# Moving the last step's burst of value products and sum products behind slot 15 of an attention kernel, with part of VectorE's end work moved forward and one key chunk's addition moved from the matrix engine to the adders

## The reference, cut to what matters

```python
Q, K, V = (split_heads(x @ W.T + b) for W, b in ((Wq, bq), (Wk, bk), (Wv, bv)))   # x: 8 x 512 x 512, 16 heads of 32
cQ = Q + split_heads(cond @ Wq.T + bq)           # cond: one row of 512 for each batch
cK = K + split_heads(cond @ Wk.T + bk)
attn = softmax(cQ @ cK.T / sqrt(32))             # 512 x 512 for each of 8 x 16 heads
out = x + attn @ V                               # float32 throughout
```

## Time and profile before

| | |
|---|---|
| median of three runs | 641.79 us |
| the profiled execution | 641.36 us |
| its span, first to last instruction | 639.5 us |
| granted TensorE clock over the span | 1.000 |
| PE busy | 633.6 us (99%) |
| DVE busy | 541.9 us (85%) |
| POOL busy | 490.6 us (77%) |
| ACT busy | 391.2 us (61%) |

### The profile page before, as it was taken

One profiled execution on the slowest core, in us unless ns is written; L12 is line 12 of the kernel. 1 busy time (PEld: TensorE's weight loads), 2 busy tenths in 40 slices (PEclk: granted clock), 3 DMA queues, 4 the chain that ended last, 5 costly groups with the idle time before them and its releaser, 6 DMA issues.

```text
span 639.5 us, 10063 instructions
## 1 busy us (share of the span) xinstructions
PE 633.6 (99%) x3528; PEld 439.5 (69%) x3528; DVE 541.9 (85%) x818; ACT 391.2 (61%) x684; POOL 490.6 (77%) x204
## 2 busy tenths in 40 slices
PE   8999999999999999999999999999999999999997
PEld 6787677666677666677666677666777666776542
DVE  7887888888888898888888888888888888998696
ACT  6466566666566666567666566565666555564773
POOL 7348877778877778877778877778877778666992
PEclk9999999999999999999999999999999999999999
DMA  8944434455434565334565334565334665424501
GB/s 262 264 101 118 116 102 114 121 151 150 108 106 106 132 151 149 103 105 102 146 151 138 105 102 108 150 152 134 101 102 117 150 166 135 117 69 120 148 17 67
DMA packets 48243, 80.83 MB, mean 126 GB/s; under 512 B 9545, under 2 KB 9801, under 8 KB 48073
## 3 DMA queue, kind: packets, MB, share of 16 engines
q1 hardware_dynamic: 47837, 80.04, 48.3%
q10 hardware_dynamic: 356, 0.16, 0.1%
HBM read 19.95 MB, written 8.39 MB: 44 GB/s over the span
## 4 chain that ended last, share of the span: by engine, by line
PE 98%; DVE 1%; DMA 0%; ACT 0%; POOLq 0%; issue 0%; DVEq 0%; ACTq 0%
PE bank L351 27%; PE bank L444 19%; PE bank L426 18%; PE bank L464 18%; PE bank L399 14%; PE bank L495 1%; DMA cond<-condT 0%; PE bank L472 0%; DVE bank L746 0%; PE bank L376 0%; POOLq L81 0%; DVE Xl L717 0%; ACT Xh L589 0%; DVE rr L784 0%; DVE rr L795 0%
## 5 line engine op out<-in xcount | busy, mean ns | idle before, releaser
L642 ACT ACTIVATE Pt<-bank 128x512 f32<-128x512 f32 x512 | 302.0, 600 | 224.0 <-PE bank L444 156.7
L746 DVE TENSOR_REDUCE mf<-bank 128x1 f32<-128x512 f32 x496 | 330.7, 684 | 59.6 <-PE bank L426 57.7
L954 POOL TENSOR_TENSOR A<-A,Pt 128x2048 f32<-128x2048 f32 x59 | 271.3, 4598 | 4.6
L444 PE MATMUL bank<-Qs,Ks 128*128 128x512 f32 x496 | 195.1, 399 | 0.1
L426 PE MATMUL bank<-Ks,Qs 128*128 128x512 f32 x496 | 194.5, 393 | 0.2
L954 POOL TENSOR_TENSOR A<-Pt 128x2048 f32<-128x2048 f32 x30 | 138.4, 4613 | 25.6 <-DVE part_sums L771 20.1
L444 PEld LDWEIGHTS bank<-Qs,Ks 128*128 128x128 f32 x496 | 92.6, 188 | 48.3 <-ACT Pt L642 26.2
L464 PE MATMUL bank<-Pt,V 128*32 128x512 f32 x1024 | 119.0, 596 | 0.0
L426 PEld LDWEIGHTS bank<-Ks,Qs 128*128 128x128 f32 x496 | 93.0, 188 | 24.0 <-DVE bank L746 3.0
L351 PE MATMUL bank<-Xh,Wh 128*128 128x512 f32 x256 | 99.8, 390 | 0.3 <-ACT Wh L581 0.3
L351 PE MATMUL bank<-Xl,Wh 128*128 128x512 f32 x256 | 100.0, 391 | 0.0
(11 more groups left out here) (74 smaller groups left out, 392.8 us busy)
## 6 DMA issues: line engine op xcount, KB each, us to landing
Qs<-hi SPq DMA_DIRECT2D x60, 256.0 KB
Ks<-hi SPq DMA_DIRECT2D x60, 256.0 KB, 3.9
Qs<-lo SPq DMA_DIRECT2D x30, 256.0 KB
Ks<-lo SPq DMA_DIRECT2D x30, 256.0 KB, 3.9
xr<-xT SPq DMA_DIRECT2D x28, 256.0 KB, 2.7
res<-xT SPq DMA_DIRECT2D x28, 256.0 KB, 2.9
outT<-ot SPq DMA_DIRECT2D x28, 256.0 KB, 3.5
Qs<-mt SPq DMA_DIRECT2D x122, 4.0 KB
```

Source lines behind the costliest of these rows:

```text
L444: e.matmul(st_bank(u)[:, :], k[:, j, kc * P:(kc + 1) * P], q[:, j, :], start=True, stop=True).then_inc(t_st, 1)
L642: e.activation(exponentials(g)[:, kc, j, :], st_bank(u)[:, :], ACT.Exp, scale=SCALE).then_inc(a_e, 1)
L746: e.reduce_max(to[:, 4 * j + qc:4 * j + qc + 1], MXB[u % 2][:, :], AXX).then_inc(v_mx, 1)
L954: e.tensor_tensor(sums, ex[:, 0, :, :] if kc == 1 else sums, ex[:, kc, :, :], ALU.add).then_inc(p_a, 1)
```

## The change

Six things are changed.

1. The burst in step 31 (values of chunks 0 and 1, sums of step 30) stands behind the scores of slot 15 in place of slot 12's.
2. `last_sums(30)` is one chunk's products in place of two: all four chunks are added up before it. To that end DVE adds chunks 0 and 1 of step 30 (`add_first(30)`, right behind the turned maxima of step 31), and POOL adds chunks 2 and 3 to it, waiting for DVE (`v_a`). POOL has two additions for step 30, as before.
3. `last_sums(31)` takes the chunks in the order 2, (0+1), 3 in place of (0+1), 2, 3.
4. PE's totals of step 27 move from slot 13 of step 30 to slot 2 of step 29, between the values of chunks 0 and 1.
5. DVE's finish of step 27 moves to step 29, slot 2, and
6. its key sums of step 28 to step 29, slot 12. Both stood behind the last reduction.

```diff
--- before.py
+++ after.py
@@ -70,11 +70,11 @@
 
 END_VALUES_AT = ((2, 12), (13,), (1, 8))
 END_TURN_AT = 2
-END_SUMS_AT = 12
-POOL_ADDS = 2
+END_SUMS_AT = 15
+END_FINISH_AT, END_KEY_SUMS_AT = 2, 12
 END_BANKS = ((1, 4, 3), (2, 12, 4))
 LAST_EARLY = (0, 1)
-LAST_ORDER = (0, 2, 3)
+LAST_ORDER = (2, 0, 3)
 
 
 def cond_attention(nc, xT, condT, wqT, wkT, wvT, biasT, outT):
@@ -481,22 +481,19 @@
 
             def last_sums(g, parts):
 
+                e.wait_ge(v_f, finished(G - 3, FIN if g == G - 1 else 1))
                 for kc in parts:
-                    if kc == 0:
-                        if g == G - 1:
-                            e.wait_ge(v_f, finished(G - 3, FIN))
-                            e.wait_ge(v_a, 1)
-                        else:
-                            e.wait_ge(v_f, finished(G - 3, 1))
-                            e.wait_ge(p_a, 3 * g + POOL_ADDS)
+                    if kc == 0 and g == G - 1:
+                        e.wait_ge(v_a, 2)
+                    elif kc == 0:
+                        e.wait_ge(p_a, 3 * g + 2)
                     else:
                         e.wait_ge(a_e, st_unit(g, kc, 3))
                     for j in range(4):
                         m = e.matmul(sums_bank(g)[32 * j:32 * j + 32, :], ones[:, :],
                                      added_up(g)[:, j, :] if kc == 0 else exponentials(g)[:, kc, j, :],
-                                     start=(kc == 0), stop=(kc == KC - 1))
-                if KC - 1 in parts:
-                    m.then_inc(t_l, 1)
+                                     start=(kc == parts[0]), stop=(kc == parts[-1]))
+                m.then_inc(t_l, 1)
 
 
             warm_up()
@@ -557,11 +554,17 @@
                     elif i < 0:
                         pass
                     elif i == 0 and n == END_VALUES_AT[i][0]:
-                        values(t - 1, (0, 1, 2, 3) if len(END_VALUES_AT[i]) == 1 else (0, 1))
+                        values(t - 1, (0,))
+                        e.wait_ge(v_mx, u - 1)
+                        totals(G - 5, MXB[u % 2])
+                        held = G - 5
+                        values(t - 1, (1,))
+                    elif i == 1 and n == END_VALUES_AT[i][0]:
+                        values(t - 1, range(KC))
                     elif n == END_VALUES_AT[i][0]:
                         values(t - 1, (0,))
                         end_totals(t - 3)
-                        values(t - 1, (1, 2, 3) if len(END_VALUES_AT[i]) == 1 else (1,))
+                        values(t - 1, (1,))
                     elif n in END_VALUES_AT[i] and t < G - 1:
                         values(t - 1, (2, 3))
                     elif n in END_VALUES_AT[i]:
@@ -570,7 +573,7 @@
                         values(t - 1, (3,))
                     if t == G - 1 and n == END_SUMS_AT:
                         values(G - 1, LAST_EARLY)
-                        last_sums(G - 2, (0,) + tuple(range(POOL_ADDS + 1, KC)))
+                        last_sums(G - 2, (0,))
             last_sums(G - 1, LAST_ORDER)
             values(G - 1, tuple(range(len(LAST_EARLY), KC)))
 
@@ -785,10 +788,12 @@
                 e.wait_ge(v_s, g + G - 1)
                 e.reciprocal(rc[:, :], rr[:, :].rearrange("p (n i) -> p n i", i=32)[:, :, 0]).then_inc(v_f, 1)
 
-            def add_first():
-                e.wait_ge(v_s, 2 * (G - 3))
-                e.wait_ge(a_e, st_unit(G - 1, 1, 3))
-                e.tensor_tensor(added_up(G - 1), Pt2[:, 0, :, :], Pt2[:, 1, :, :], ALU.add).then_inc(v_a, 1)
+            def add_first(g):
+
+                e.wait_ge(v_s, 2 * (g - 2))
+                e.wait_ge(a_e, st_unit(g, 1, 3))
+                ex = exponentials(g)
+                e.tensor_tensor(added_up(g), ex[:, 0, :, :], ex[:, 1, :, :], ALU.add).then_inc(v_a, 1)
 
             def inverse_turned(g):
                 e.wait_ge(v_f, finished(g, 1))
@@ -829,6 +834,12 @@
                 e.wait_ge(d_res_last, 64)
                 e.scalar_tensor_tensor(out[:, HALF:S], O[:, HALF:S], vb[:, c, b:b + 1], res_rows(g)[:, HALF:S],
                                        ALU.add, ALU.add).then_inc(v_f, 1)
+
+            def finish(g, bk):
+                sums_inverted(g, bk)
+                inverse_turned(g)
+                normalised(g)
+                added(g)
 
             e.memset(res[:, 0:256], 0.0).then_inc(v_c, 1)
             e.memset(cT[:, :, :], 0.0).then_inc(v_c, 1)
@@ -881,27 +892,24 @@
                         added(g)
                     if (g := projected(t, n, K_LO_AT, EARLY_K_LO_AT)) is not None:
                         qk_lo(1, g)
+                    if (t, n) == (G - 3, END_FINISH_AT):
+                        finish(G - 5, MXB[u % 2])
+                    if (t, n) == (G - 3, END_KEY_SUMS_AT):
+                        key_sums(G - 4, 0)
+                        key_sums(G - 4, 1)
                     if t < G - 3 and (g := due(t, n, SUMS_AT[0], -1)) is not None:
                         key_sums(g, 0)
                     if t < G - 3 and (g := due(t, n, SUMS_AT[1], -1)) is not None:
                         key_sums(g, 1)
 
-            def finish(g):
-                sums_inverted(g, MXB[0])
-                inverse_turned(g)
-                normalised(g)
-                added(g)
-
             last_parts()
             maxima_turned(G - 1)
-            key_sums(G - 4, 0)
-            key_sums(G - 4, 1)
-            finish(G - 5)
+            add_first(G - 2)
             key_sums(G - 3, 0)
             key_sums(G - 3, 1)
-            finish(G - 4)
-            finish(G - 3)
-            add_first()
+            finish(G - 4, MXB[0])
+            finish(G - 3, MXB[0])
+            add_first(G - 1)
             last_sums_inverted(G - 2)
             inverse_turned(G - 2)
             normalised(G - 2)
@@ -943,12 +951,12 @@
                 elif kc == 1 and g == G - 3:
 
                     e.wait_ge(t_vj, G)
-                elif kc == 1 and g == G - 2:
-                    e.wait_ge(v_s, 2 * (G - 4))
                 elif kc == 1 and g >= 1:
                     e.wait_ge(v_s, 2 * g)
-                if kc > 1:
-                    e.wait_ge(p_a, 3 * g + kc - 1)
+                if g == G - 2 and kc == 2:
+                    e.wait_ge(v_a, 1)
+                elif kc > 1:
+                    e.wait_ge(p_a, 3 * g + kc - (2 if g == G - 2 else 1))
                 e.wait_ge(a_e, st_unit(g, kc, 3))
                 sums, ex = added_up(g), exponentials(g)
                 e.tensor_tensor(sums, ex[:, 0, :, :] if kc == 1 else sums, ex[:, kc, :, :], ALU.add).then_inc(p_a, 1)
@@ -990,8 +998,8 @@
             add(G - 3, 1)
             add(G - 3, 2)
             add(G - 3, 3)
-            for kc in range(1, POOL_ADDS + 1):
-                add(G - 2, kc)
+            add(G - 2, 2)
+            add(G - 2, 3)
             half = out_rows(G - 1)[:, 0:HALF]
             e.wait_ge(a_rb, 1)
             e.wait_ge(v_h, 1)
```

## The result

The changed kernel took 643.14 us against 641.79 (medians of seven runs each): ratio 1.0029, 95% interval 1.0019 to 1.0039, so 1.35 us slower. The profiled execution took 644.62 us, its span 642.8; it is the longest of the seven, and what its opening adds has to be separated first.

A forecast was written before the change was run, and what follows sets the result against it. PE bounds the kernel (99% busy), DVE close behind in the last step. A 0.8 us delay from step 29 plus the burst made the last transpose +0.94 us late: 641.79 + 0.94 = 642.7 us, range 641.3 to 643.7.

The forecast's parts named there:

- the first hole: DVE's 1.60 us idle time in step 29; the moved 2.44 us finish makes the next reduction 0.79 us late.
- Rival (d): At the moved finish of step 27: it pushes more than its overhang, +1.3 to +1.8 us; chance 0.12.
- The second hole: DVE's 2.28 us idle time in step 29; the 2.33 us key sums of step 28 cost 0 there.
- The burst: Step 31: scores 13 to 15 stall at ACT's pace, eating the 0.86 us saved by one chunk of sums fewer.
- the +0.1 of the prediction: Parts 1 to 3 of the change, with no delay from further up: worth +0.1 us.
- DVE decides: At the end of step 31: DVE's 3.28 us finish of step 30, not PE's last sums, sets the last transpose.
- `add_first(30)`: DVE's addition in the end list: runs 2.28 us from about 614.9 and costs 0.
- the case with exclusion: `add_first(30)` in DVE's end list: held until POOL's addition ends at 617.0, ends at 619.3; costs nothing given 0.6 us slack.
- the base sum: The delays followed to the last transpose: it starts at 634.80 in place of 633.86, +0.94 us.
- Rival (a): DVE's queue, 625 to 631: late residual, or DVE and POOL exclude each other without slack; +1.4 to +2.4 us; chance 0.18.
- the +0.5 to +1.28 of the forecast: The band of slowdown in us given to the forecast for the whole kernel, with chance 0.45.

The follow-up runs named there:

- e8: The kernel before with only the totals and finish of step 27 moved to slot 2 of step 29; 642.62 against 641.71 us, ratio 1.0012.
- e2: The changed kernel with the key sums of step 28 back in DVE's end list; 642.64 against 641.70 us for the kernel before, ratio 1.0013.
- e1: The changed kernel with the finish of step 27 and its totals back in their old places; 642.74 against 641.70 us for the kernel before, ratio 1.0014.
- e4: The kernel before with only the burst moved from behind slot 12 to behind slot 15; 643.09 against 641.70 us, ratio 1.0019.
- e9: The changed kernel with step 30's last addition moved from DVE to POOL; 641.93 against 641.58 us for the kernel before, ratio 1.0004.
- e6: e5 with POOL's last addition for step 30 left out; 640.67 against 641.58 us for the kernel before, ratio 0.9984.
- e5: The changed kernel, burst behind slot 12, finish 27's multiplication and addition back in DVE's end list; 641.77 against 641.58 us for the kernel before, ratio 1.0002.

## Why the prediction was right

It said 642.7 us (+0.9), and it was 643.14 (+1.35). In the trace the last transpose came +1.17 us late, where the sum had +0.94. The path was the forecast one: late from the first hole on, and DVE's finish of step 30 in front of the last transpose. The sizes of two of its terms were short.

- **The first hole.** 0.79 predicted, 0.84 measured, 0.74 at the end when alone (e8). The residual was just in time, as said, with some 0.06 us of wait. Rival (d), that the finish pushes more than its overhang, did not happen (2.44 - 1.60 is 0.84), though the measured +1.35 lies in the band that it was given.
- **The second hole.** 0 predicted, 0.01 measured, and e2 shows that the key sums cost nothing in the end list either. That what both moves free is worth nothing holds for them, but not for the finish of 27: e1 ended 0.74 us later than taking back the delay alone would have it, through the wait for its totals and POOL's later additions.
- **The burst.** Sums of step 30 ready +1.22 predicted, +1.40 measured. The mis-sized term is the end of score 15: I took 0.25 us from its start to the values' start, but from its load (630.57) to the values' first product (631.07) it is 0.50. The kernel before had shown it: there a score that waited for ACT has its load at 623.07, and the load of the values behind it is at 623.50, 0.43 us later, as far apart as 630.57 and 631.00.
```profile
623.07 0.19 PEld L444 LDWEIGHTS bank<-Qs,Ks 128*128 128x128 f32 x1 [0.30 <-ACT Pt L642]
```
With it parts 1 to 3 alone come to more than the +0.1 of the prediction: 1.17 - 0.85 = 0.32 by subtraction, 0.38 by e4.
- **DVE decides.** 3.33 predicted between the transposes, 3.38 measured, and PE's sums aren't waited for; e9 shows it by taking 0.79 us out of DVE's part.
- **`add_first(30)`.** It took 4.57 us in place of 2.28, and cost nothing, as the case with exclusion said. I had the base sum without it. The Trainium skill (SBUF — State Buffer, "Who interferes with whom") states that a VectorE instruction with two SBUF inputs contends with a GpSimd instruction that reads SBUF, by an exclusive lock. All sixteen VectorE additions of this size that met a running POOL addition, in the changed kernel and the runs, agree with it: they ended 2.14 to 2.16 us behind POOL's end, whether they had begun 2.4 (617.06) or 0.2 us (e2) before it. Rival (a) is this mechanism with the slack gone; the slack was 0.74 us, where I had 0.6.
- **The chances.** I gave 0.63 to a change of less than 0.2% and 0.32 to more. The ratio of 1.0029 is in the second, less likely class, though its interval begins at 1.0019. The direction was forecast, and the size is 0.4 us short of the median; by the trace's +1.17 it is inside the +0.5 to +1.28 of the forecast, by the median just outside.

What I said of part 2 of the change, that its saving is lost because DVE isn't there to take the sums, holds with the burst behind slot 15. With the burst behind slot 12 e6 against e5 shows another reason: since the saving is bought with a VectorE addition for which POOL has to wait, POOL is still adding when VectorE's next addition is due, and holds it.

## What to carry to other kernels

Before work is moved into an engine's idle gap, compare its length with the gap: 2.44 us in 1.60 cost the difference in full, 2.33 us in 2.28 cost nothing, and the first part of the same work alone (1.0 us) fitted (e5: 0.07). Look at what the work held up in its old place too: put back there, it cost almost as much (e1). A product burst placed behind producers that are paced by another engine loses the cover that it gave them. When a cheap chain gets shorter in front of an engine, see how long that engine is from its own start to the next: here 3.38 us of VectorE stood between two inversions, so PE's saved 0.86 us found nobody to take it, while one 0.75 us addition moved to GpSimd took 0.79 us out between the two (e9).

## What the hardware showed that I had not expected

- VectorE waits for the whole of GpSimd's addition: its own 2.28 us addition took 4.57, 4.24, 3.48 and 2.96 us, in each case until 2.15 us behind the end of GpSimd's. I had taken 2.28 as the base and 0.18 us as the only sign. Whether GpSimd waits as exactly for a VectorE addition that began first is not shown: in these runs semaphores kept its additions behind, and in rows 10, with 0.33 us of VectorE's left, it took 0.18 us longer.
- The opening moves the whole execution: 2.15 us between two traces of the same code at 34 to 36 us, more than the effect that was measured. A late load and a slow stretch of products both had a part in it. Only times from a common anchor behind it could be compared.
